# Two attention layers on one core: layer 0's chunk reordered, layer 1's q and k kept by halves of a head's dimension

## The reference, cut to what matters

```python
# layer 0: scores = q.k * scale, softmax, .v, output projection; FFN with ternary weights
# layer 1:
q = _rope(q, c, s)            # t1*c - t2*s, t1*s + t2*c over the two halves of the 64
k = _rope(k, c, s)
kb = -p * jnp.log1p(a * dist) # a bias per head and distance
attn = softmax(q.k * SCALE + kb)
out = (attn @ v) @ out_w.T    # FFN: one of 8 experts per row, chosen by a router
```

## Time and profile before

| what | value |
|---|---|
| time, median of 3 runs | 2997.02 us (2996.97 to 2999.35) |
| the profiled execution | 2997.32 us, span 2995.6 us |
| busy in the span | PE 91%, DVE 82%, ACT 53%, POOL 82% |
| DMA, mean | 52 GB/s, 18.0% of 16 engines on SP's queue |

### The profile page before, as it was taken

One profiled execution on the slowest core, in us unless ns is written; L12 is line 12 of the kernel. 1 busy time (PEld: TensorE's weight loads), 2 busy tenths in 40 slices (PEclk: granted clock), 3 DMA queues, 4 the chain that ended last, 5 costly groups with the idle time before them and its releaser, 6 DMA issues. The chain is left out here.

```text
span 2995.6 us, 46382 instructions
## 1 busy us (share of the span) xinstructions
PE 2729.9 (91%) x17528; PEld 1133.6 (38%) x17528; DVE 2459.0 (82%) x3309; ACT 1588.5 (53%) x1972; POOL 2458.6 (82%) x1186
## 2 busy tenths in 40 slices
PE   5959999999999999998588299999999999999996
PEld 3413333333333333333354033333333333333333
DVE  6568888888888888884566499999999999999994
ACT  3325555555555555554154155555555555555554
POOL 0009999999999999998244389999999999999997
PEclk8979999999999999999699599999999999999998
DMA  4250111111111111100323502211112121221100
GB/s 112 88 197 10 31 30 31 29 31 30 30 30 31 29 31 30 30 3 1 93 82 112 168 9 56 56 56 56 56 56 56 56 57 56 56 56 56 56 1 15
DMA packets 66063, 155.26 MB, mean 52 GB/s; under 512 B 17697, under 2 KB 31402, under 8 KB 63666
## 3 DMA queue, kind: packets, MB, share of 16 engines
q1 hardware_dynamic: 64818, 150.20, 18.0%
q0 software_dynamic: 1024, 2.10, 0.2%
HBM read 113.34 MB, written 38.93 MB: 51 GB/s over the span
## 5 line engine op out<-in xcount | busy, mean ns | idle before, releaser
L947 POOL TENSOR_TENSOR a_sums<-a_sums,room 128x1024 f32<-128x1024 f32 x512 | 1194.9, 2362 | 66.3 <-ACT room L788 42.2
L699 PE MATMUL a_ov<-room,va 128*64 128x512 f32 x4096 | 994.6, 606 | 0.0
L777 ACT ACTIVATE room<-room,sscale 128x1024 f32<-128x1024 f32 x512 | 588.8, 1150 | 504.3 <-DVE room L877 504.3
L844 DVE TENSOR_REDUCE a_mx<-a_jb 128x1 f32<-128x1024 f32 x501 | 611.8, 1221 | 128.9 <-PE a_jb L653 122.7
L947 POOL TENSOR_TENSOR a_sums<-room 128x1024 f32<-128x1024 f32 x256 | 603.2, 2357 | 76.2 <-ACT room L781 49.6
L839 DVE CUSTOM_DVE_ANT_0 a_junk<-a_jb,a_tab 128x1024 bf16<-128x1024 f32 x501 | 609.8, 1217 | 62.2 <-DVE a_m L850 36.1
L877 DVE TENSOR_TENSOR room<-a_st,a_tab 128x1024 f32<-128x1024 f32 x512 | 623.8, 1220 | 14.1 <-PE a_st L688 12.9
L788 ACT ACTIVATE room<-a_st,sscale 128x1024 f32<-128x1024 f32 x256 | 285.0, 1113 | 359.3 <-PE a_st L688 359.3
L652 PE MATMUL a_jb<-a_kh,a_qh 64*128 64x512 f16 x1002 | 387.0, 386 | 41.5 <-DVE a_mx L844 25.9
L688 PE MATMUL a_st<-a_qh,a_kh 64*128 64x512 f16 x2048 | 390.8, 378 | 0.0
L688 PE MATMUL a_st<-a_ql,a_kh 64*128 64x512 f16 x2048 | 390.0, 378 | 0.0
(11 more groups left out here) (231 smaller groups left out, 2470.3 us busy)
## 6 DMA issues: line engine op xcount, KB each, us to landing
a_tab<-bias_line SPq DMA_DIRECT2D x16, 1984.0 KB
a_qh<-qk_high SPq DMA_DIRECT2D x64, 256.0 KB, 4.5
a_kh<-qk_high SPq DMA_DIRECT2D x64, 256.0 KB, 5.0
a_ql<-qk_low SPq DMA_DIRECT2D x64, 256.0 KB, 6.6
a_kl<-qk_low SPq DMA_DIRECT2D x64, 256.0 KB, 6.8
qk_high<-q_oh SPq DMA_DIRECT2D x16, 512.0 KB, 2.6
qk_low<-q_ol SPq DMA_DIRECT2D x16, 512.0 KB, 3.6
qk_high<-er_split SPq DMA_DIRECT2D x32, 256.0 KB
```

Source lines behind the costliest of these rows:

```text
L699: last = nc.tensor.matmul(ov[t * DH:(t + 1) * DH, :], k.va[:, 2 * s + t, h * DH:(h + 1) * DH], prob[:, step % RING, t * QC:(t + 1) * QC], ...
L777: nc.scalar.activation(prob[:, r, :], prob[:, r, :], ACT.Exp, scale=k.sscale[:, layer:layer + 1])\
L844: nc.vector.reduce_max(mx[:, j // 2, j % 2:j % 2 + 1], scratch(n, j), AX.X).then_inc(max_done, 1)
L947: nc.gpsimd.tensor_tensor(a, first, prob[:, step % RING, :], ALU.add).then_inc(summed, 1)
```

## The change

1. Layer 0's chunk. `row` stands after step 3 and `sums_of` after step 5 (before: 5 and 3). On DVE, `maxima` comes ahead of `subtract_maxima` in an odd step. On ACT, `divide_maxima(n + 1)` stands ahead of the exponent of step 0 (before: behind that of step 2), `copy_out` behind step 0 (before: step 1), `row` behind step 2 (before: step 5).
2. The code for both layers is now one, and with it ACT's `row` of layer 1 stands behind the exponent of step 2, where it stood behind that of step 3.
3. Layer 1's q and k lie in DRAM by halves of the head's dimension: the first halves of all heads, then the second. `rows_of` gives 128 successive rows. Layer 1's loads fetch each half of a head by itself: 16 transfers of 32 rows a head, where there were 8 of 64.
4. ACT reads a tile's owner in `pick`, not all 23 ahead.

```diff
-SUM_STEP, ROW_STEP, OUT_STEP = (3, 5), (5, 3), (7, 7)
+SUM_STEP, ROW_STEP, OUT_STEP = 5, 3, 7
+DR = DH // 2
+def by_halves(store):
+    return store.rearrange("a p s -> (a p) s").rearrange("(r x) s -> r x s", r=2)
+        low_loads = 8 if bias else 4
+        loads = low_loads + (1 if bias else 0)
+        def placed(h):
+            pr, half = h // 2, slice((h % 2) * DH, (h % 2 + 1) * DH)
+            for low in (0, DH):
+                if not bias:
+                    yield slice(low, low + DH), lambda store: store[pr][half, :]
+                else:
+                    for r in range(2):
+                        yield (slice(low + r * DR, low + (r + 1) * DR),
+                               lambda store, r=r: by_halves(store)[r, h * DR:(h + 1) * DR, :])
...
@@ PE @@
             def row(n):
                 pe.wait_ge(m4_done, n + 1)
-                if bias and n >= 3:
+                if n >= 3:
                     pe.wait_ge(proj_done, n - 2)
-                if not bias and n >= 2:
-                    pe.wait_ge(rs_done, n - 1)
             def sums_of(n):
                 pe.wait_ge(folded, n + 1)
-                pe.wait_ge(row_done, min(n + (3 if bias else 2), NCH))
+                pe.wait_ge(row_done, min(n + 3, NCH))
@@ ACT @@
-                    if bias and s == 0 and n + 1 < NCH:
+                    if s == 0 and n + 1 < NCH:
                         divide_maxima(n + 1)
                     exponent(n, s)
-                    if s == (0 if bias else 1) and n >= 1:
+                    if s == 0 and n >= 1:
                         copy_out(n - 1)
-                    if not bias and s == 2 and n + 1 < NCH:
-                        divide_maxima(n + 1)
-                    if s == row_step and n + 1 < NCH:
+                    if s == ROW_STEP - 1 and n + 1 < NCH:
                         row(n + 1)
@@ DVE @@
-                    if not by_row(NS * n + s):
-                        subtract_maxima(n, s)
                     if n + AHEAD < NCH:
                         maxima(n + AHEAD, s)
                     if bias:
                         add_bias(n, s)
+                    elif not by_row(NS * n + s):
+                        subtract_maxima(n, s)
@@ SP, rotation @@
-                rows = store[i].rearrange("a p s -> (a p) s").rearrange("(g h r d) s -> g r h d s", g=4, h=4, r=2)
-                return [rows[g, r, :, :, half * 1024:(half + 1) * 1024] for r in range(2)]
+                rows = by_halves(store[i])
+                return [rows[r, g * P:(g + 1) * P, half * 1024:(half + 1) * 1024] for r in range(2)]
@@ ACT, experts @@
-            owners = [act.value_load(tiles[0:1, i:i + 1], min_val=0, max_val=NE - 1) for i in range(TL)]
             def pick(i):
+                owner = act.value_load(tiles[0:1, i:i + 1], min_val=0, max_val=NE - 1)
```

More of the change, by code:

```diff
@@ L598, in attention_stage @@
                                                                                    if bias else None)
-        sum_step, row_step, out_step = SUM_STEP[layer], ROW_STEP[layer], OUT_STEP[layer]
         lowered = None if bias else m.sem(g + "lowered")
         st_read = added if bias else exp_done
-        loads = 4 + (1 if bias else 0)
+        low_loads = 8 if bias else 4
+        loads = low_loads + (1 if bias else 0)
         FIRST = AHEAD * NJ
@@ L622, in _ @@
                     sp.wait_ge(loaded, 16 * loads * h)
-                    sp.wait_ge(low_loaded, 16 * 4 * h)
+                    sp.wait_ge(low_loaded, 16 * low_loads * h)
                 if h >= 2:
@@ L626, in _ @@
                 at = slice((h % 2) * S, (h % 2 + 1) * S)
[L627 to L630, removed]
+                for to, rows in placed(h):
+                    sp.dma_start(qh[to, at], rows(k.qk_high[0])).then_inc(loaded, 16)
+                    sp.dma_start(kh[to, at], rows(k.qk_high[1])).then_inc(loaded, 16)
                 if bias:
@@ L634, in _ @@
                     sp.wait_ge(loaded, 16 * loads)
-                for low in (slice(0, DH), slice(DH, P)):
-                    sp.dma_start(ql[low, at], k.qk_low[0, pr][half, :]).then_inc(low_loaded, 16)
-                    sp.dma_start(kl[low, at], k.qk_low[1, pr][half, :]).then_inc(low_loaded, 16)
+                for to, rows in placed(h):
+                    sp.dma_start(ql[to, at], rows(k.qk_low[0])).then_inc(low_loaded, 16)
+                    sp.dma_start(kl[to, at], rows(k.qk_low[1])).then_inc(low_loaded, 16)
         @block.tensor
@@ L673, in scores @@
                 if n % NC == 0 and s == 0:
-                    pe.wait_ge(low_loaded, 16 * 4 * (n // NC + 1))
+                    pe.wait_ge(low_loaded, 16 * low_loads * (n // NC + 1))
                 if step >= 2 and by_row(step):
@@ L733, in between @@
             def between(n, s):
-                if s == row_step and n + 1 < NCH:
+                if s == ROW_STEP and n + 1 < NCH:
                     row(n + 1)
-                if s == sum_step and n >= 1:
+                if s == SUM_STEP and n >= 1:
                     sums_of(n - 1)
-                if s == out_step and n >= 1:
+                if s == OUT_STEP and n >= 1:
                     project(n - 1)
@@ L814, in _ @@
                 for s in range(NS):
-                    if bias and s == 0 and n + 1 < NCH:
+                    if s == 0 and n + 1 < NCH:
                         divide_maxima(n + 1)
                     exponent(n, s)
-                    if s == (0 if bias else 1) and n >= 1:
+                    if s == 0 and n >= 1:
                         copy_out(n - 1)
-                    if not bias and s == 2 and n + 1 < NCH:
-                        divide_maxima(n + 1)
-                    if s == row_step and n + 1 < NCH:
+                    if s == ROW_STEP - 1 and n + 1 < NCH:
                         row(n + 1)
-                    if bias and s == out_step and n >= 1:
+                    if bias and s == OUT_STEP and n >= 1:
                         scale(n - 1)
@@ L908, in _ @@
                         add_bias(n, s)
-                    if s == sum_step and n >= 1:
+                    elif not by_row(NS * n + s):
+                        subtract_maxima(n, s)
+                    if s == SUM_STEP and n >= 1:
                         invert(n - 1)
-                    if not bias and s == out_step and n >= 1:
+                    if not bias and s == OUT_STEP and n >= 1:
                         accumulate(n - 1)
@@ L1356, in _ @@
         def _(act):
-            owners = [act.value_load(tiles[0:1, i:i + 1], min_val=0, max_val=NE - 1) for i in range(TL)]
             act.wait_ge(weights_loaded, 16 * (1 + FT))
             def pick(i):
-                nc.scalar.activation(w1i[:, i % 2, :], w1[:, bass.ds(owners[i], 1), :].rearrange("p a f -> p (a f)"),
+                owner = act.value_load(tiles[0:1, i:i + 1], min_val=0, max_val=NE - 1)
+                nc.scalar.activation(w1i[:, i % 2, :], w1[:, bass.ds(owner, 1), :].rearrange("p a f -> p (a f)"),
                                      ACT.Copy).then_inc(picked, 1)
```

## The result

The changed kernel takes 2920.74 us, the median of 4 runs (2920.11 to 2923.89), where the kernel before took 2997.86 beside it. The ratio is 0.974, with a 95% interval of 0.973 to 0.976. The predicted time was 2927.

The account below looks back on a forecast made before the run. No engine saturated everywhere: layer 0 bound by a jb-maxima chain and PE, layer 1 by late sums, the rotation by slow stores on SP's queue. 2997 - 41 + 1 - 14 - 16 = 2927 us; 8-in-10 range 2900 to 2957.

Parts of the forecast that it names:

- the two chunk terms: Layer 0's chunk order and layer 1's earlier ACT row, forecast to save 14 and 16 us.
- The forecast's own range: 2912 to 2942 us: rotation saving 33 to 46, layer 0 from 6 to 22, layer 1 from 8 to 20.
- Term 1: Rotation: stores in 128 rows hold SP's queue at most 1 us, ending ACT's and DVE's waits; 41 us saved.
- Owners read in `pick` at 0: Layer 0 experts' stage: ACT's 23 owner reads between copies fit in its free time; 0 us.
- Term 2: Layer 1's loads: sixteen instead of eight a head, only the first head exposed; +1 us.
- Term 3: Layer 0's chunk: maxima first shortens the chain from 4.35 to 3.98 us; chunk 18.62 to 18.40, 14 us saved.
- The wait of jb for the maxima nearly gone: Expected in the next profile of layer 0, with pairs without extras at 4.0 to 4.2 us.
- Term 4: Layer 1: ACT's row one exponent earlier lets sums start 0.26 us sooner a chunk; 16 us saved.
- POOL absorbing the chunk terms: Rival: POOL or DVE absorbs both chunk gains, leaving 2957 us; chance 0.10.
- slow stores: Rival: the write or source, not the shape, limits the rotation's stores, giving 2968 us; chance 0.05.
- The fast rival: Layer 0 reaches PE's own time (34 us), layer 1 its whole gap (24), rotation 43: 2896 us; chance 0.10.
- The slower rival: Layer 0's odd exponents come too late and stop PE ahead of `values`; 3067 us at 0.5 a pair; chance 0.03.

Follow-up runs that it names:

- experiment 1: Changed kernel with layer 1's q and k stores and loads in the old layout (4x32x1024 stores, 8 loads of 64 rows a head); 2964.84 us.
- experiment 5: Kernel before with only layer 1's q and k stored in 128 rows and loaded by halves; 2955.37 us, ratio 0.986.
- experiment 11: Changed kernel with ACT again reading the 23 tile owners ahead of everything in the layer 0 experts' stage; 2919.39 us, ratio 0.973.
- experiment 3: Changed kernel with DVE's subtraction ahead of the maxima again in layer 0, the rest of the new order kept; 2940.37 us.
- experiment 9: Kernel before with only the swap of row and sums in layer 0 (row in step 3, sums in step 5); 2994.91 us, ratio 0.999.
- experiment 8: Kernel before with only DVE's maxima ahead of the subtraction in layer 0, row and sums left in steps 5 and 3; 3112.07 us, ratio 1.038.
- experiment 4: Changed kernel with two buffers for the eight partial maxima, so a chunk's first reduction needn't wait for DVE's merge; 2914.11 us, ratio 0.972.
- experiment 2: Changed kernel with ACT's row of layer 1 back behind the exponent of step 3, nothing else; 2934.99 us, ratio 0.979.
- experiment 6: Kernel before, old DRAM layout and loads kept, each store cut in four (one head, 32x1024, 64 KB each); 2959.51 us, ratio 0.987.
- experiment 7: Kernel before, old DRAM layout and loads kept, each store cut in two (two heads, 2x32x1024, 128 KB each); 3159.36 us, one run.

## Why the prediction was right, point by point

**The sum.** 70 us were forecast, and the span fell by 77.3: rotation 41.8 (41 forecast), loads -0.2 (-1), layer 0's chunks 17.2 (14), layer 1's row 13.0 (16), and 5.5 that no term had (4.0 at the end of layer 0, 1.5 at the start). Each mechanism is shown by its own experiment, but part of the closeness is luck: the errors of the two chunk terms, +3 and -3, cancel. The forecast's own range doesn't follow from its terms either: their ends, with the loads at +1, add up to 2910 and 2951, not to 2912 and 2942.

**Term 1, the rotation: 41 predicted, 41.8 on the trace, 44 by experiments 1 and 5.** By its own steps: jobs at 8.45 us each were to put job 12 15.2 us earlier in the stage. PE's first group of that job and DVE's last operation after the change:

```profile
1577.39 1.02 PE L1296 MATMUL er_low_part<-room,wo 128*128 128x512 f32 x2
...
1618.58 1.73 DVE L1445 TENSOR_TENSOR er_split<-er_second,er_split 128x1024 f16<-128x1024 f32 x1 [3.38 <-ACT er_split L1402]
```

Against the first load of layer 1 (1622.90 and 1687.37) job 12 starts 45.5 us ahead, where it was 72.0: 26.5 of the gain lie behind it, and 15.3 ahead of it, as laid out. Jobs 2 to 12 follow each other at 8.39 us. From job 12's start to DVE's end it is 42.9 us where the sum had 41: jobs 12 to 15 take 11.3, 7.2, 8.4 and 16.0, for 11, 8, 8 and 14, so it is the last job that was laid out too short. From there to the first load it is 2.6 where it had 4: two errors of under 2 us that nearly cancel. Of the 2 to 3 us between trace and experiments most is spread between runs: by the spans of their profiled executions the same experiments 1 and 5 give 42.9 and 42.7. The 2.75 us a store that the prediction reads from the earlier trace rows is 2.45, by the caution above. Owners read in `pick` at 0: consistent with experiment 11.

**Term 2, the loads: +1 predicted, 0.2 measured.** SP issues a half of a head in 0.3 to 0.4 us, and the first high load is followed by the first low load, which waits for the high parts and the bias table, after 12.8 us, from 12.6. The figures for small transfers that the prediction cites from the Trainium skill (DMA: Bandwidth & Descriptors, "Bandwidth") had no effect of their size: 4.5 us was the estimate. The table alone is 1984 KB of what lands in that time, and it lands last.

```profile
1622.90 0.32 SPq L645 DMA_DIRECT2D a_qh<-qk_high  x1
1623.27 0.42 SPq L646 DMA_DIRECT2D a_kh<-qk_high  x1
...
1626.82 0.34 SPq L648 DMA_DIRECT2D a_tab<-bias_line  x1
1635.69 0.31 SPq L652 DMA_DIRECT2D a_ql<-qk_low  x1
```

**Term 3, layer 0's chunk: 18.62 to 18.40 predicted, 18.33 measured.** The mechanism held, and three of the four pairs to 0.01 us. The mis-sized one is pair (0,1), 4.12 for 4.19: from `accumulate` to the next chunk's reduction I had read 1.29 in the earlier trace rows, where DVE had waited for jb at its end; with DVE as the late one it is 1.22 (641.17 to 642.39). The term gives 17.2 us, for 14. Left out altogether was the end of layer 0, 4.0 us: there PE has no maxima, reaches step 3 early and waited for POOL's total. That is the swap's doing: with the swap and the old order on DVE (experiments 3 and 9) the last three intervals still sum to 46.4, for 51.2.

That 4.0 has 1.7 us of the clock in it. In the kernel before, PE waits 1.11 us for the total at 1381.95; from 1382.85 to 1386.00 its granted clock is 0.52, and the products take 3.62 us. In experiment 5, whose layer 0 is the same code, the same wait of 1.10 us is followed by a granted clock of 1.00 and products of 1.94, and the three intervals sum to 49.37. So the same layer 0 code has this cost in some executions and not in others.

The swap stands in that term in half a sentence, that sums no longer stand right behind POOL's total. The timeline shows what it is worth, first before, then after:

```profile
654.53 1.27 POOL L954 TENSOR_TENSOR a_total<-a_sums 128x512 f32<-128x512 f32 x1
```

```profile
647.49 1.27 POOL L966 TENSOR_TENSOR a_total<-a_sums 128x512 f32<-128x512 f32 x1
...
652.21 1.05 PE L724 MATMUL a_xb<-ones,a_total 128*128 128x1 f32 x8
```

Before, the total ends at 655.80 and sums starts at 655.98, 0.18 later. After, it ends at 648.76 and sums starts at 652.21, which leaves 3.4 us of room. At sums' old place, 0.31 behind the odd jb of step 3 (647.65), the total would be 0.8 late (experiment 8 measured 1.05). The total has come later against PE's steps, as the odd exponents have, and 0.18 us was all the cover there was. The half sentence carries the term: without it the change of order on DVE costs 112 us. I laid out the chain with the sums moved, so the sum was right; but I hadn't seen how much hung on the swap: experiment 8's expectation has the wait for the total, and still says 2985 to 2997 for a kernel that took 3112. "The wait of jb for the maxima nearly gone" was wrong as well: it is 103.2 us from 600 to 1200, from 155.7. Most of these are waits of the weight load's queue beside a PE that still works. Not all of them are free, though: pair (0,1) is 4.12 us where PE's own time is 3.92, and experiment 4 took 0.13 of that off while PE's busy time hardly rose, from 598.9 to 600.0.

**Term 4, layer 1's row: 16 predicted, 13.0 on the trace (12.8, and 0.2 for the loads), 14 by experiment 2.** The term was 0.26 by 62; the gap shrank by 0.22, from 0.38 to 0.16 and not to 0.12, and the chunk is 19.315 us for 19.28.

**The rivals and the signs.** POOL absorbing the chunk terms is ruled out by the two chunk periods (ACT's even exponent waits 0.5 us a chunk for POOL's ring slot, which is new and hides), slow stores by experiments 1 and 5 to 7. The fast rival, with 34 and 24 us for the two chunk terms, got half of each. The slower rival, late odd exponents, never came near in the changed kernel: no wait of the values for an odd exponent shows in mid layer 0. ACT's `copy_out` doesn't hold up the exponent of step 1 either, but only just: the subtraction ahead of that exponent ends at 646.46, and the exponent starts 0.03 us later, as it does in the other odd steps, while the copy started at 645.98. The danger lay one step further on, in the total that POOL makes of those exponents, and there it has 3.4 us of room only because of the swap. The rivals priced it at the wrong place.

## What to carry to other kernels

A reordering that looks like two independent edits has to be costed as a square: here one edit was worth -4 us, the other +112, and both together -22. When work on one engine is put later, follow what it feeds to the next engine that waits in order, not only to the first. When stores are slow while the DMA engines are mostly idle, look at the outermost dimension of the transfer before anything else; these runs varied the destination's. And where a wait enters a loop of TensorE, price the clock behind it too.

## What the runs showed of the hardware that was not expected

An idle microsecond of PE ahead of a run of products was followed, in some chunks and not in others of the same kernel, by about 3 us at 1.2 GHz (granted clock 0.58, then 0.50), which cost more than the wait: 1.56 us against 1.05. In experiment 8 that is 35 chunks of 60, in the turn of eight given there. The head's loads don't decide which: in the 3.1 us from 702.49 on the granted clock is 0.52 with a DMA share of 0.00, and from 723.64 on it is 1.00 with a share of 0.99. What does isn't settled.

Cutting a store in two pieces of the wrong shape made each piece hold SP's queue as long as the whole had (2.44 us for 128 KB with two packets in flight, 2.45 for 256 KB with four), while cutting it in four made the four together hold the queue for less than the one (4 x 0.43 us).

After the change one place that still waits long is the start of layer 1, where PE idles 24 us and the first head's bias table ends the wait; before it was 43.9. Of the 24, 11.1 lie ahead of the first load, while DVE, ACT and SP finish the rotation, and 12.9 are the first head's loads and the table, which is issued last of them. No run tried to shorten it.

```profile
1635.81 0.58 PE L668 MATMUL a_st<-a_kh,a_qh 64*128 64x512 f16 x1 [24.05 <-DMA a_tab<-bias_line]
```
